# A cross-batch attention stage in a new layout: scores with channels on partitions, summed over channels by column-tiled products on TensorE, and no products on GpSimd

## What is computed

```
qkv = x @ in_proj_w.T + in_proj_b ; q, k, v = split(qkv)      # T,B,C = 8,256,128
q, k, v = reshape to (8, 256, 16, 8)
scores = einsum('tbhd,sbhd->bhts', q, k) * 8**-0.5
attn = softmax(scores, axis=-1)
ctx = einsum('bhts,sbhd->tbhd', attn, v).reshape(T, B, C)
h = layernorm(x + ctx @ out_w.T + out_b, ln1)
logits = h @ router_w.T + router_b ; assign = max(top2 indices)
out[t] = w2[assign] . gelu(w1[assign] . h + b1) + b2
result = layernorm(h + out, ln2)
```

## Time and profile before

| | |
|---|---|
| median of 3 runs | 1094.59 us (1093.68 to 1095.0) |
| profiled execution | 1097.17 us, span 1095.1 us |
| granted TensorE clock, mean of the span | 0.852 |
| TensorE busy (matmul) | 807.3 us, 74% |
| VectorE busy | 668.3 us, 61% |
| ScalarE busy | 366.5 us, 33% |
| GpSimd busy | 374.5 us, 34% |

### The profile page before, as it was taken

The page is one execution under the profiler, slowest core; times in us unless marked ns, Lnnn a source line. Parts: engine busy times, 40 slices in busy tenths (PEclk is TensorE's granted clock), DMA queues, the critical chain, the costliest instruction groups (busy, mean ns, idle before and its releaser), DMA issues.

```text
span 1095.1 us, 14546 instructions
## 1 busy us (share of the span) xinstructions
PE 807.3 (74%) x5027; PEld 546.9 (50%) x5027; DVE 668.3 (61%) x1842; ACT 366.5 (33%) x729; POOL 374.5 (34%) x512
## 2 busy tenths in 40 slices
PE   2718999257888788867094698399989897994384
PEld 1717888133444444433094476166634574774373
DVE  5682222366877877737968567877457437896421
ACT  1123444036655555641000343165400133442210
POOL 5324331575444433008536301200200002534254
PEclk9757999569989999998597699599889898997588
DMA  8507774100000000000000000000000050001221
GB/s 210 203 13 204 204 211 135 29 15 10 11 9 9 1 2 1 1 1 1 0 1 1 0 1 1 0 1 1 1 0 0 1 153 1 2 1 58 73 62 32
DMA packets 51771, 45.44 MB, mean 41 GB/s; under 512 B 6805, under 2 KB 47656, under 8 KB 51443
## 3 DMA queue, kind: packets, MB, share of 16 engines
q1 hardware_dynamic: 48146, 36.91, 11.5%
q0 software_dynamic: 3552, 7.61, 2.7%
HBM read 36.90 MB, written 7.80 MB: 41 GB/s over the span
## 4 chain that ended last, share of the span: by engine, by line
PE 57%; DVE 23%; issue 7%; POOL 6%; ACT 4%; DMA 2%; POOLq 0%; SPq 0%; DVEq 0%; ACTq 0%
PE psum L2333 5%; PE psum L1071 3%; PE psum L1963 3%; PE psum L1362 3%; DVE XN L155 3%; PE psum L2523 2%; PE psum L1991 2%; PE psum L1982 2%; PE psum L2553 2%; DVE stats L141 2%; PE psum L1276 2%; PE psum L1339 2%; PE psum L560 2%; DVE scratch L1603 2%; DVE scratch L1821 2%
## 5 line engine op out<-in xcount | busy, mean ns | idle before, releaser
L1603 DVE TENSOR_REDUCE scratch<-psum 128x2 f32<-128x512 f32 (+1 forms) x160 | 107.7, 686 | 63.2 <-PE psum L1319 40.7
L1521 ACT ACTIVATE scratch<-psum 128x512 f32<-128x512 f32 x160 | 94.1, 603 | 95.3 <-PE psum L1339 93.8
L196 POOL TENSOR_SCALAR veps<-moments 128x4 f32<-128x4 f32 x44 | 8.5, 194 | 328.0 <-DVE moments L144 324.1
L232 PE MATMUL psum<-ident,XN 128*128 128x128 f32 x144 | 32.8, 373 | 83.9 <-DVE XN L155 67.1
L232 PEld LDWEIGHTS psum<-ident,XN 128*128 128x128 f32 x144 | 22.4, 192 | 91.5 <-DVE XN L155 44.3
L243 ACT ACTIVATE XT<-psum 128x512 f32<-128x512 f32 x36 | 21.2, 597 | 129.6 <-PE psum L232 129.6
L852 DVE SCALAR_TENSOR_TENSOR scratch<-psum,b_block_bias,scratch 128x256 f32<-128x256 f32 (+1 forms) x48 | 18.6, 430 | 74.3 <-ACT scratch L996 69.9
L919 POOL DMA_INDIRECT scratch<-pair_rows,b_gather_at x39 | 39.2, 1004 | 71.5 <-PE psum L1044 44.8
L2333 PE MATMUL psum<-late,scratch 128*128 128x512 f32 x128 | 58.0, 615 | 5.7 <-DVE routing_wide L2276 5.0
L2457 POOL TENSOR_TENSOR scratch<-scratch,arena 128x1024 f32<-128x1024 f32 x16 | 30.4, 1901 | 91.8 <-DVE arena L2677 91.8
L1319 PE MATMUL psum<-arena 128*128 128x512 bf16 x128 | 52.8, 421 | 5.4 <-ACT arena L1501 3.5
(11 more groups left out here) (437 smaller groups left out, 2067.9 us busy)
## 6 DMA issues: line engine op xcount, KB each, us to landing
arena<-in_L_ffn_w SPq DMA_DIRECT2D x72, 128.0 KB
arena<-in_L_ffn_wg SPq DMA_DIRECT2D x24, 256.0 KB
wide<-in_L_xattn_Wkv SPq DMA_DIRECT2D x1, 2048.0 KB
wide<-in_L_ffn_W SPq DMA_DIRECT2D x1, 2048.0 KB, 8.7
late<-in_L_ffn_W SPq DMA_DIRECT2D x8, 256.0 KB, 7.0
pair_results<-scratch SPq DMA_DIRECT2D x15, 128.0 KB
X<-in_x SPq DMA_DIRECT2D x2, 512.0 KB, 5.1
C<-in_ctx SPq DMA_DIRECT2D x2, 512.0 KB, 6.4
```

Source lines behind the costliest of these rows:

```text
L232: last = t.transpose(c.bank[self.banks[g % 2]][:, i * P:(i + 1) * P], self.src[:, GROUP * g + i, :], c.ident[:])
L1521: a.activation(out, bank[3 + e % 2][:, :], ACT.Exp).then_inc(s["exp"], 1)
L1603: v.tensor_reduce(out, bank[m % 3][:, :].rearrange("p (h t) -> p h t", t=n), AX.X, ALU.max, negate=True).then_inc(s["maxed"], 1)
```

## The change

Queries and keys are made transposed: `Win` is the weight and a whole group of `XT` (512 columns) moves, so that channels lie on partitions and positions along the free dimension. The queries' and keys' bias is then one number a partition (`b_qk`, two more loads) and is added in the copy out of PSUM. Values are made as before, with the bias by a product of one row. Each score product is one VectorE instruction over 8 x 128 elements of 128 channels. TensorE sums over the 8 channels of a head with a 0/1 matrix (`head8`) of 32 columns that is put at column tile r = t // 2; even and odd t share a tile, with the matrix shifted by 16 columns. Two tokens of different tiles are summed together. Scores of (t, h) then lie on partitions and positions along the free dimension, so the maximum and the sum over s are folds of whole tiles. The weights are transposed back (8 transposes for each m), and the value products read them from PSUM. A value product is folded once on VectorE (1024 to 512) and TensorE sums four pieces, not eight. The order of VectorE's and TensorE's work is the list `ORDER`. GpSimd keeps the inverse roots and adds `b_out` group by group; the next stage's `prepare` and the shift of `X` wait until `moe` has reached `NG`.

```diff
+        c.head8 = c.sb("head8", [P, 48])
...
+        own.link(g, g.memset(c.head8[:], 0.0))
+        own.link(g, g.memset(c.head8[:, 16:32], 1.0))
+        select(c.head8[:, 16:32], [[-8, 16]], 0, 1)
+        select(c.head8[:, 16:32], [[8, 16]], 7, -1)
...
-    POOL_SCORES, POOL_VALUES = (0, 2, 4, 5, 7), (1, 4, 7)
+    ORDER = (("S", 0, 0), ("S", 0, 2), ("S", 0, 4), ("S", 0, 6), ("S", 0, 1), ("S", 0, 3), ("S", 0, 5), ("S", 0, 7),
+             ("S", 1, 0), ("S", 1, 2), ("V", 0, 0), ("S", 1, 4), ("S", 1, 6), ("V", 0, 1), ("V", 0, 2),
+             ("S", 1, 1), ("S", 1, 3), ("V", 0, 3), ("V", 0, 4), ("S", 1, 5), ("S", 1, 7), ("V", 0, 5), ("V", 0, 6),
+             ("V", 0, 7), ("V", 1, 0), ("V", 1, 1), ("V", 1, 2), ("V", 1, 3), ("V", 1, 4), ("V", 1, 5), ("V", 1, 6),
+             ("V", 1, 7))
+    PAIR_BANK = (2, 3, 0, 1)
...
+    def score_product(self, v, m, t, u):
+        rows = slice(m * P, m * P + P)
+        q = self.qT.rearrange("p (t x) -> p t x", t=8)[:, t, rows]
+        return v.tensor_tensor(self.prod[:, u, :].rearrange("p (s x) -> p s x", s=8), bc(q[:, None, :], (P, 8, P)),
+                               self.kT.rearrange("p (s x) -> p s x", s=8)[:, :, rows], ALU.mult)
+    def value_product(self, v, m, t, u):
+        w = self.c.psum[:, 4 + 2 * m:6 + 2 * m, :].rearrange("p k (s n) -> p (k s) n", s=4)[:, :, 16 * t:16 * t + 16]
+        return v.tensor_tensor(self.prod[:, u, :].rearrange("p (s h c) -> p s h c", s=8, c=8),
+                               bc(w[:, :, :, None], (P, 8, 16, 8)),
+                               self.v[:, :, m, :].rearrange("p s (h c) -> p s h c", c=8), ALU.mult)
...
     def pool(self, g):
+        for q in range(NG):
+            self.norm.turn.wait(g, q + 1)
+            tiles = c.XN[:, GROUP * q:GROUP * q + GROUP, :]
+            g.tensor_tensor(tiles, tiles, bc(self.b_out[:, None, :], (P, GROUP, D)), ALU.add).then_inc(s["biased"], 1)
         self.ln1.pool(g)
-        g.wait_ge(s["reduced"], 16)
+        g.wait_ge(s["moe"], NG)
...
     def dve(self, v):
+        for g in range(NG):
+            v.wait_ge(s["proj"], (1, 2, 3, 5)[g])
+            v.tensor_scalar(self.kT[:, g * CHUNK:(g + 1) * CHUNK], c.bank[g][:, :], self.b_qk[:, 1:2], None, ALU.add) \
+                .then_inc(s["k_copied"], 1)
+        def fold(op, values):
+            own.link(v, v.tensor_tensor(self.half, values[:, 0:4, :], values[:, 4:8, :], op))
+            own.link(v, v.tensor_tensor(self.quarter, self.half[:, 0:2, :], self.half[:, 2:4, :], op))
+            own.link(v, v.tensor_tensor(self.one, self.quarter[:, 0, :], self.quarter[:, 1, :], op))
         def shift(m):
+            v.wait_ge(s["used"], self.number("S", m, 7))
+            scores = c.psum[:, 2 * m:2 * m + 2, :].rearrange("p k (s x) -> p (k s) x", s=4)
+            own.link(v, v.tensor_copy(self.half, scores[:, 0:4, :]))
+            own.link(v, v.tensor_tensor(self.half, self.half, scores[:, 4:8, :], ALU.max))
...
+            v.tensor_tensor(self.w[:, m], scores, bc(self.one[:, None, :], (P, 8, P)), ALU.subtract) \
...
         def divide(m):
             v.wait_ge(s["exp"], m + 1)
+            fold(ALU.add, self.w[:, m])
+            own.link(v, v.reciprocal(self.one, self.one))
+            v.tensor_tensor(self.w[:, m], self.w[:, m], bc(self.one[:, None, :], (P, 8, P)), ALU.mult) \
...
+        for n, (kind, m, t) in enumerate(self.ORDER):
+            if n >= 4:
+                v.wait_ge(s["used"], n - 3)
+            if kind == "S":
+                v.wait_ge(s["copied"], t // 2 + 1)
+                self.score_product(v, m, t, n % 4).then_inc(s["made"], 1)
+            else:
+                if t == 0:
+                    v.wait_ge(s["copied"], 2 * NG)
+                    v.wait_ge(s["w_turned"], m + 1)
+                own.link(v, self.value_product(v, m, t, n % 4))
+                half = self.prod[:, n % 4, 0:512]
+                v.tensor_tensor(half, half, self.prod[:, n % 4, 512:1024], ALU.add).then_inc(s["made"], 1)
+            if (kind, m, t) == ("S", 0, 7):
+                shift(0)
+            if (kind, m, t) == ("S", 1, 2):
+                divide(0)
+            if (kind, m, t) == ("V", 0, 5):
+                shift(1)
+            if (kind, m, t) == ("V", 0, 6):
+                divide(1)
...
     def pe(self, t):
+        def keys(g):
+            turns.wait(t, g + 1)
+            t.matmul(c.bank[g][:, :], self.Win[:, D:2 * D], c.XT[:, g * CHUNK:(g + 1) * CHUNK],
+                     start=True, stop=True).then_inc(s["proj"], 1)
+        def vals(g):
...
+            for i in range(GROUP):
+                j, at = GROUP * g + i, slice(i * D, (i + 1) * D)
+                t.matmul(out[:, at], c.XT[:, j * P:(j + 1) * P], self.Win[:, 2 * D:3 * D], start=True, stop=False)
+                last = t.matmul(out[:, at], c.ones[0:1, :], self.b_in[0:1, 2 * D:3 * D], start=False, stop=True)
+        def score_sums(n):
+            pair = self.ORDER[n:n + 2]
+            t.wait_ge(s["made"], n + 2)
+            for half in range(2):
+                for i, (_, m, tok) in enumerate(pair):
+                    r, odd = tok // 2, tok % 2
+                    last = t.matmul(c.bank[2 * m + half][32 * r:32 * r + 32, :],
+                                    c.head8[:, 0:32] if odd else c.head8[:, 16:48],
+                                    self.prod[:, (n + i) % 4, half * 512:(half + 1) * 512],
+                                    start=not odd, stop=bool(odd), tile_position=(0, 32 * r))
+            last.then_inc(s["used"], 2)
...
+        def value_sums(n):
...
+            for i in range(4):
+                last = t.matmul(out, self.prod[:, n % 4, i * D:(i + 1) * D], c.ident[:], start=(i == 0), stop=(i == 3))
+            last.then_inc(s["used"], 1)
...
+        turns.pe_group(t, 0)
+        turns.pe_group(t, 1)
+        keys(0)
+        turns.pe_group(t, 2)
+        keys(1)
+        keys(2)
+        queries(0)
+        turns.pe_group(t, NG - 1)
+        keys(NG - 1)
+        for g in range(1, NG):
+            queries(g)
+        for g in range(NG):
+            vals(g)
...
+            if (m, tok) == (0, 0):
+                turn_weights(0)
+            if (m, tok) == (0, 7):
+                turn_weights(1)
+            value_sums(n)
+            n += 1
+            if m and tok >= 2 and tok % 2 == 0:
+                project_out(tok // 2 - 1)
+        project_out(NG - 1)
```

More of the change, by code:

```diff
@@ L1737, in __init__ @@
         self.own = c.dve_chain
-        self.dve_values = [t for t in range(8) if t not in self.POOL_VALUES]
-        self.dve_order = [8 * m + t for m in range(2) for t in self.dve_values]
-        self.s = c.signals("d", "qkv qkv_first copied prod scored shifted exp attn prod_v prod_w reduced out residual "
+        self.s = c.signals("d", "proj k_copied copied made used shifted exp attn w_turned biased out residual "
                                 "h_affine pick "
@@ L1850, in dve @@
[L1850 to L1859, removed]
+            fold(ALU.add, self.w[:, m])
+            own.link(v, v.reciprocal(self.one, self.one))
+            v.tensor_tensor(self.w[:, m], self.w[:, m], bc(self.one[:, None, :], (P, 8, P)), ALU.mult) \
+                .then_inc(s["attn"], 1)
+        v.wait_ge(s["k_copied"], NG)
@@ L1966, in pe @@
-        t.wait_ge(s["copied"], 8)
-        for j in range(NT):
-            t.wait_ge(s["copied"], 8 + j // GROUP + 1)
-            last = t.matmul(c.bank[j // 4][:, (j % 4) * D:(j % 4 + 1) * D], c.XT[:, j * P:(j + 1) * P],
-                            self.Wout[:], start=True, stop=True)
-            if j % 4 == 3:
-                last.then_inc(s["out"], 1)
+        turns = self.norm.turn
+        def keys(g):
+            turns.wait(t, g + 1)
+            t.matmul(c.bank[g][:, :], self.Win[:, D:2 * D], c.XT[:, g * CHUNK:(g + 1) * CHUNK],
+                     start=True, stop=True).then_inc(s["proj"], 1)
@@ new lines, in turn_weights @@
+        def turn_weights(m):
+            t.wait_ge(s["attn"], m + 1)
+            if m == 0:
+                t.wait_ge(s["copied"], 2 * NG)
+            for at in range(8):
+                last = t.transpose(c.bank[4 + 2 * m + at // 4][:, at % 4 * P:(at % 4 + 1) * P], self.w[:, m, at, :],
+                                   c.ident[:])
+            last.then_inc(s["w_turned"], 1)
+        def value_sums(n):
+            _, m, tok = self.ORDER[n]
+            t.wait_ge(s["made"], n + 1)
+            if (m, tok) == (1, 4):
+                t.wait_ge(s["copied"], 2 * NG + 2)
+            if m:
+                out = c.bank[self.PAIR_BANK[tok // 2]][:, tok % 2 * P:(tok % 2 + 1) * P]
+            else:
+                out = c.bank[tok // 4][:, tok % 4 * P:(tok % 4 + 1) * P]
+            for i in range(4):
+                last = t.matmul(out, self.prod[:, n % 4, i * D:(i + 1) * D], c.ident[:], start=(i == 0), stop=(i == 3))
+            last.then_inc(s["used"], 1)
@@ new lines, in project_out @@
+        def project_out(q):
```

(10 more changed lines are left out.)

168 lines of the change are left out of this document (61 added, 107 removed).

## The result

The changed kernel takes 1098.86 us (median of 20 runs, 1093.12 to 1100.78) against 1094.88 us (20 runs) of the kernel before on the same chips: a ratio of 1.0033, 95% interval 1.0024 to 1.0042. It is slower by a third of a per cent, where 14.8 us less were forecast.

The account below looks back on a forecast made before the run. VectorE bounds the scores and TensorE the value sums, one after the other. The attention's -10.5 us and -4.3 behind it sum to -14.8, so 1094.6 becomes 1079.8 us; range 1073 to 1088.

Parts of the forecast that it names:

- group 3 normalized, turned, copied: Start of the attention: four normalizations held by GpSimd, 2.0 us instead of 1.1, then turn 1.1 and ScalarE's copy 0.6.
- mixed part and half 1: Attention from the first value product: value products 1.91 us each with fold, VectorE leading and TensorE keeping up, together 44.85 us.
- behind the attention, difference: Moving GpSimd's preparation behind `moe` frees VectorE's normalizations, 7.92 to about 4.3 us; the second turn comes 4.3 us sooner.
- one row saves nothing: Value projection: a one-row product costs as much as a full one, so 32 products at 0.22 us take 7.1.
- from here on: Clock: with key products in the gap, TensorE runs at 1.00 from the projections on, except behind pauses of several us.
- Rival D: Whole attention: TensorE stays at clock 0.50, costing 10.5, 5.5 and about 7 us, giving 1102.8 us; chance 0.04.
- A: Score sums: column tiles in pairs don't overlap, a pair costs 3.5 us, 6.1 us more, giving 1085.9; chance 0.09.
- B: Expert rounds: GpSimd's moved work stretches VectorE there and the gain is given back, 1086.9 us; chance 0.05.
- C: Value products: read from PSUM and repeated over channels, they run at half pace, 19.8 us more, 1099.6; chance 0.04.
- L573's block: Behind the attention: freeing L573 from GpSimd gives nothing, covered by ScalarE's table spreading; worth 3.9 us without that cover.
- The rule that was weighed: Score and value sums: tiling-mode changes drain the engine; at 0.2 us each, 1080.4 us, but the trace shows no gap.
- plus 0.15 as there: Score sums: 0.15 us, taken from L1362, added to the 1.7 of a pair's four products, making 1.85.

Follow-up runs that it names:

- experiment 1: Changed kernel, but the values' bias product has 128 rows (a matrix of 1/128) instead of one; 1085.17 us, 0.9906 of the kernel before.
- experiment 2: Changed kernel, but one one-row bias product of 512 columns per group, ahead of its four value products; 1084.7 us, 0.9906 of the kernel before.
- experiment 4: Changed kernel, but GpSimd adds `b_out` only when all four groups are turned; 1090.74 us, 0.996 of the kernel before.

## Why the prediction was wrong

The miss is 18.3 us in the attention: forecast -10.5, measured +7.8. By the steps of the prediction, with its times taken from VectorE's start with group 3:

| step | forecast us | measured us |
|---|---|---|
| group 3 normalized, turned, copied | 3.7 | 5.5 (487.36 to 492.88) |
| key and query products | 3.4 | 6.4 (to 499.24) |
| value projection | 7.1 | 18.4 (to 517.66) |
| first four pairs of sums | 8.5 | 11.9 (to 529.60) |
| `shift`, two products, `divide`, weights turned | 11.45 | 10.9 (to 540.47) |
| mixed part and half 1 | 44.85 | 44.2 (to 584.70) |
| residual | 7.06 | 7.05 |
| behind the attention, difference | -4.3 | -4.5 |

*The projections: this step failed.* It said that "one row saves nothing" and stopped there, with 0.91 for a pair of L1949's records beside 0.67 at L1991's pace. That difference was the answer. In the kernel before the half without one-row products gives VectorE a tile every 0.63 us (five L1802 in 3.14 us from 497.72), the half with them makes a product every 0.84, so each change cost 0.2 already. The 0.91 was read with its tail; from start to start it is 0.84. With 384 columns that is a quarter; with 128 columns and a change at every product it doubles the product, 0.22 to 0.42. Experiments 1 and 2 show this: 32 x 0.2 = 6.4 of the 11.3 us.

*The clock: the other 4.9 us there, some 2.6 at the key and query products and 3.4 at the first sums. This step failed too.* The prediction took 1.00 "from here on", because TensorE would be busy. In the changed kernel it was busy in all records from 499.2 to 517.7 and the clock fell after 6.2 us. The same products at full pace (experiment 1) kept it, and so did the kernel before with the same alternation at 384 columns:

```profile
500.80:513.50 12.70, 12.70 (x31) 4.42 (x30) 10.23 (x10) 3.43 (x7) 12.00 (x5) 1.00 0.00 0
```

That the sums' 3.4 us were the clock is shown by experiment 1 as well, where they took 1.9 us a pair, 8.6 for all four pairs, and VectorE led. What makes the clock fall in the alternation stays open. Rival D, clock lost over the whole attention, was priced at 23 us and given 0.04; it happened in part, by a cause that the rival did not name.

*Group 3: right in kind, mis-sized.* It was charged 0.49 us a tile from rows beside short GpSimd instructions; beside additions of 1.26 us a tile took 1.0 on average. By the single records the first three tiles took 1.3 us each, one addition beside each, and the fourth, with none beside it, 0.34. This also made TensorE's pause 3.2 us long and not 0.3 as in experiment 4, and the next four products then ran at 0.50 for the most part: 6.4 us, 3.8 there. Experiment 4 shows both together, 5.6 us.

*The rest held.* Value products out of PSUM, folds, the softmax, the overlap of column tiles, the mixed part where VectorE leads, the preparation moved behind `moe`, and next to no cost in the expert rounds (0.3 us): each within 1 us. Rivals A, B and C did not occur. That L573's block was covered by ScalarE's spreading held too: L586 came at 612.61 with its cover, 4.7 us behind the router's end, before 4.8.

*The rule that was weighed.* The prediction looked for the cost of a change of tiling mode at the column tiles and wrote that the trace shows no such gap. It does. In the changed kernel a pair of sums in column tiles is followed by a value sum on the full array (128*128 in the records):

```profile
550.75 1.91 PE L1985 MATMUL psum<-scratch,head 128*32 128x512 f32 x8 [1.11 <-DVE scratch L1772]
552.60 1.16 PE L2011 MATMUL psum<-ident,scratch 128*128 128x128 f32 x8
...
576.53 1.06 PE L2020 MATMUL psum<-d_Wout,XT 128*128 128x128 f32 x8
```

L2011 begins 1.85 us behind the pair, whose four products are 1.72 at their pace of 0.43, and its eight records last 1.16 us, where eight such records behind others of the full array last 1.06 (L2020). That is 0.2 us for the change, as much as between 128 rows and one. The row that the prediction read has it as well: the 1.0 us of L1362 against 0.85 is this for the most part, and with the "plus 0.15 as there" it stood in the price of a pair under the name of a tail. Since VectorE leads in the mixed part, it changed nothing there. By the Trainium skill, TensorEngine Tiling (Array Packing), Key Properties, a change of tiling mode drains the engine; the trace agrees at the column tiles. Whether a product of one row among products of 128 is such a change, that section does not say; the equal price speaks for it, and no run here decides it.

## What to carry to other kernels

When a product is made smaller, divide what the old trace charges for each *product*, not for each column: a row that is longer than its columns explain holds a fixed cost, and here it was 0.2 us at each change between 128 rows and one, or between the full array and column tiles. A bias of one row is not free on TensorE; put it where it is one number a partition, or make it once for a group. And a GpSimd instruction let in early should run beside VectorE instructions that read PSUM (three key copies 2.07 us with it and without), since a normalization from SBUF to SBUF (1.3 us instead of 0.34) and a product of two SBUF operands (2.29 instead of 1.2) waited until the addition in flight had ended.

## What the runs showed of the hardware

A TensorE that is busy in every record can lose its clock: 0.50 from 505.4 to 517.7 us, behind 6.2 us with a product of 128 columns each 0.42 us, half of them of one row. With a product each 0.22 us (experiment 1, 7.2 us long), with 512 columns in the one-row products (experiment 2, 8.6 us long) or with 384 in all (the kernel before, 12.7 us) it stayed at 1.00. What in the alternation brings the fall is not settled by these runs: in experiment 2 the one-row products took half of the time too, and it stayed.

A change between 128 rows and one row costs 0.2 us in both directions (experiment 2), and so does one from column tiles of 32 to the full array (1.85 us instead of 1.72 up to L2011, 1.16 instead of 1.06 in it). The other way, the first sums of experiment 1 begin 0.32 us behind the start of the last bias product (506.51 to 506.83), where 0.22 is its pace.

Column tiles work side by side: four fp32 products of 512 columns took 3.62 us in one tile and 1.91 in two, and eight took 1.94 in four.
